# Mamba scan with a mixture-of-experts layer: z products in slot 9, the next x transposed in slot 58, the last state's quarters scaled by ScalarE and summed on TensorE

## The chip, the cores and the metric

The kernel runs on one core of one Trainium2 chip. The metric is the device time of one execution in microseconds. The core's engines are TensorE (PE; PEld is its weight load), VectorE (DVE), ScalarE (ACT), GpSimd (POOL) and SyncE (SP), which here issues all DMAs. Each engine runs its own list of instructions in order; semaphores tie the lists together.

## The reference

The input `x` is 2 sequences of 4096 tokens with 256 values. All is float32.

```python
x = x + layernorm(mamba(layernorm(x)))
x = x + layernorm(moe(layernorm(x)))

def mamba(x):                        # 512 inner channels, 16 states
    x_in, z = split(x @ W_in)
    u = silu(causal_conv(x_in, 4 taps) + conv_b)
    dt_lr, B, C = split(u @ W_xproj)            # 16, 16, 16
    delta = softplus(dt_lr @ W_dt + b_dt)
    A = -exp(A_log)
    h[n] = exp(delta * A[n]) * h[n] + delta * u * B[n]   # over time, for each of 16 states
    y = sum_n h[n] * C[n]
    return ((y + D_skip * u) * silu(z)) @ W_out

def moe(x):                          # 8 experts of width 128, top 2, and a shared one of 256
    coef = top-2 of softmax(x @ router)
    return shared(x) + sum_e coef[e] * (silu(x @ gate[e]) * (x @ up[e])) @ down[e]
```

## The kernel before, in words

The tokens are cut into 16 chunks of 512, 8 of each sequence, the two sequences taken in turn. Channels lie on the partitions: 512 channels are 4 blocks `j`, 512 tokens are 4 quarters `a` of 128. The kernel is a software pipeline. In body `s` the scan of chunk `s` runs; beside it run the output part and the experts of chunk `s-1` (`ffn_part`), the preparation of chunk `s+1` (`prep_part`: x and z products, convolution, delta, B, C), and the loading and normalising of `x` for chunk `s+2` (`XA`). Every body has 64 slots, and each engine's list is written out slot by slot: in slot `t` VectorE does scan `t` (state `t//4`, block `t%4`), and all other work is placed by slot numbers (`XIN_PE`, `YD_PE`, `Z_PE`, `SILU`, and so on). Nothing is planned at run time.

The scan itself: ScalarE computes `d_a = exp(delta * a)` into one of two PSUM banks (`decay`, L602, two slots ahead; it waits for the scan that last read the bank), POOL computes `d_bu` for two blocks at once (`inflow`, L987), VectorE runs the recurrence (`scan_step`, L753). When a state's 4 blocks are done, TensorE transposes each quarter into one of two `ht` banks (`transpose_state`, L445). The quarter is scaled by `C` and summed into `y_t`: the first state by ScalarE (`first_state`, L610), the other 15 by VectorE (`add_state`, L763), two in every second slot (`ADDS`), and the last state's four quarters in slots 0 and 1 of the next body (`ADDS_LATE`).

After that, in slots 2 to 9 of the next body, `y_t` is transposed back (`transpose_y`, L458, into two `RING` and two `DN` banks), VectorE adds `D_skip * u` (`skip_u`, L770, slot 3), POOL multiplies by silu(z) (`gate_y`, L1033, slot 4), TensorE projects (`project_out`, L469), VectorE takes moments (slot 8), POOL makes `rstd_o`, VectorE adds the stream and takes the next moments (slot 9, L786), ScalarE normalises (L619), TensorE transposes (L490), ScalarE copies to `x1_t` (L660). Each expert pair has a gate product, silu (L671, `silu_slot`: 14, 24, 34, 44, 52), up product, copy (L675), `hidden` on POOL (L1040, L1045) and a down product (L536) that accumulates in `DN`. In slot 60 VectorE takes the moments of y over `DN` (L774), before the adds of that slot; in slot 0 ScalarE normalises them (`normed_y`, L628), and POOL adds them to the stream (`add_stream_y`, L976, slot 7).

Preparation: `x_t` transposes the normalised `xa` (L423, slot 0), ScalarE copies it (L688, slot 1); x products (L433) go to the ring in slots 4, 7, 8; tap 0 on ScalarE (L698), the others on VectorE (L907); z products 0 and 1 in slot 9 into `DN`, 2 and 3 in slots 60 and 61 into the ring; silu of u and z (L704, L708) in slots 8, 11 and 62. ScalarE's `exp`, `silu` and `softplus` each need a table load where they follow one another; `Copy` and `Identity` don't.

Of the kernel before, what the change touches and what calls it, by code (L numbers as in the profile page):

```python
# [33 lines left out]
def mamba_moe_kernel(nc, x, w_in, conv_w, conv_b, w_xproj, w_dt, b_dt, a_log, d_skip, w_out,  # L34
# [3 lines left out]
    P = 128  # L38
# [20 lines left out]
    with ExitStack() as ctx:  # L59
# [51 lines left out]
        HF = sb("hidden", [P, 2, T])  # L111
        UP = sb("up", [P, 2, T])
# [41 lines left out]
        yd, y_first, xt = stage("yd", J), stage("y_first", NT), stage("xt", KM)  # L154
# [10 lines left out]
        scan, add_c, carry = stage("scan", NS * J), stage("add_c", (NS - 1) * NT), stage("carry_s", NS)  # L165
# [4 lines left out]
        conv, u_s, sz = stage("conv", J * TAPS), stage("u_s", J), stage("sz", J)  # L170
        RT_STEPS = 18
# [18 lines left out]
        YD_PE, YD_DVE, Y_GATE, OUT_PE = 2, 3, 4, (5, 5, 6, 6)  # L190
        Y_POOL = 7
# [12 lines left out]
        ADDS_LATE = {0: (SLOTS - NT, SLOTS - NT + 1), 1: (SLOTS - NT + 2, SLOTS - NT + 3)}  # L204
# [191 lines left out]
        def _(pe):  # L396
# [4 lines left out]
            def body(s, lo, r):  # L401
# [3 lines left out]
                for t in range(SLOTS):  # L405
# [3 lines left out]
                    for q in ADDS_LATE.get(t, ()):  # L409
                        if ffn:  # L410
                            transpose_state(s - 1, q)
                    if ffn:
                        ffn_part(s, lo, t)
                    if prep:
                        prep_part(s, lo, 1 - r, t)

            def x_t(s, lo):

                pe.wait_ge(norm["xa"].sem, norm["xa"].at(s + 1))
# [29 lines left out]
            def transpose_y(s, lo, j):  # L449

                pe.wait_ge(*added(s - 1, SLOTS - 1))
# [4 lines left out]
                bank = yd_bank(j)  # L456
                for a in range(NT):
                    last = nc.tensor.transpose(bank[:, a * P:(a + 1) * P],  # L458
                                               YT[:, a, j * P:(j + 1) * P], IDN[:, :])
# [82 lines left out]
            def prep_part(s, lo, o, t):  # L542
                c = s + 1
                if t == 0:
                    x_t(s, lo)
# [3 lines left out]
                for j in range(J):  # L549
                    if t == Z_PE[j]:  # L550
                        if j < 2:
                            pe.wait_ge(resid["o"].sem, resid["o"].at(s - 1, 2 * j + 2))
                        else:
                            pe.wait_ge(*ring_user_before(s, lo, "z", j))
                        for k in range(KM):
                            last = nc.tensor.matmul(z_bank(j)[:, :], WIN[:, k, DI + j * P:DI + (j + 1) * P],
# [31 lines left out]
        def _(act):  # L588
# [23 lines left out]

            def normed(w, c, dst, src):
# [18 lines left out]
            def body(s, lo, r):  # L632
                with_scan, ffn, prep = parts(lo)
                o = 1 - r
                for t in range(SLOTS):
# [47 lines left out]
            def prep_part(s, lo, o, t):  # L683
                c = s + 1
                if t == 1:
                    for k in range(KM):
                        act.wait_ge(full["xt"].sem, full["xt"].at(c, k + 1))
                        nc.scalar.activation(XT[:, k, :], ring_bank("xt", k)[:, :], ACT.Copy)\  # L688
# [398 lines left out]
```

## Time and profile before

| | |
|---|---|
| median of 3 runs | 2432.21 us (2432.09 to 2432.26) |
| profiled execution, its own time | 2430.07 us |
| span in the profile | 2428.1 us |
| VectorE busy | 2228.7 us, 92% |
| TensorE busy | 2073.8 us, 85% |
| GpSimd busy | 1906.6 us, 79% |
| ScalarE busy | 1601.1 us, 66% |

The span is cut into 40 slices on the page; VectorE stands at 9 tenths or more in all but the first and three of the last four. One chunk takes some 145.6 us (scan 0 of one at 1187.36 us, of the next at 1333.0 us). A line of the timeline view gives the start, the duration of a merged run of like instructions, and in brackets the idle time of that engine before it and what released it. A line without brackets followed the one before without a wait worth showing. In a merged run the instructions overlap a little: two adds of 0.73 us take 1.38.

### The profile page before, as it was taken

What the parts mean: (1) busy time and instruction counts of PE and PEld (TensorE: products, weight loads), DVE (VectorE), ACT (ScalarE), POOL (GpSimd) and SP (SyncE); (2) the same over time, 40 slices, a digit from 0 to 9 for tenths busy, and PEclk for the clock granted to TensorE, in tenths of its full rate; (3) what the DMA queues carried; (4) which work ended last, traced back from release to release, by engine and by line L of the source; (5) the groups of instructions that cost most, each with busy time, mean ns of one, the idle gap of its engine ahead of it and who ended that gap; (6) DMA issues with size and microseconds to landing.
All of it is one profiled execution on the core that took longest, in us unless ns stands there. A gap on an engine that the chain in (4) does not pass through costs nothing. (4 is left out here: it accounts for less than half of the span.)

```text
span 2428.1 us, 29696 instructions
## 1 busy us (share of the span) xinstructions
PE 2073.8 (85%) x8960; PEld 1322.8 (54%) x8960; DVE 2228.7 (92%) x3176; ACT 1601.1 (66%) x2358; POOL 1906.6 (79%) x1566
## 2 busy tenths in 40 slices
PE   5668989889898988989888898888989898896977
PEld 2445555656555555655655555555555555564544
DVE  3999999999999999999999999999999999998950
ACT  4556767676776767777677676667677676675632
POOL 3576887969789696978969788796978879698844
PEclk9659999999999999999999899999999999998989
DMA  4111211111121121111211121121112111111101
GB/s 135 34 34 42 70 53 57 58 49 57 53 62 57 49 57 58 57 53 58 65 46 47 58 65 55 55 57 50 56 53 62 61 49 53 49 57 48 65 23 44
DMA packets 92943, 134.23 MB, mean 55 GB/s; under 512 B 12000, under 2 KB 42976, under 8 KB 92784
## 3 DMA queue, kind: packets, MB, share of 16 engines
q1 hardware_dynamic: 92784, 132.34, 18.2%
q8 instruction: 72, 1.18, 0.2%
q14 instruction: 87, 0.71, 0.1%
HBM read 123.13 MB, written 9.18 MB: 54 GB/s over the span
## 5 line engine op out<-in xcount | busy, mean ns | idle before, releaser
L753 DVE TENSOR_TENSOR_SCAN h<-d_a,carry,d_bu 128x512 f32<-128x512 f32 x1024 | 1262.0, 1267 | 35.8 <-ACT d_a L602 35.4
L987 POOL TENSOR_TENSOR d_bu<-delta_u,b_rows 128x1024 f32<-128x1024 f32 x512 | 1202.3, 2357 | 5.1 <-DMA b_rows<-b_rows_hbm 0.9
L602 ACT ACTIVATE d_a<-delta,a_neg 128x512 f32<-128x512 f32 x1024 | 696.4, 689 | 622.2 <-DVE h L753 620.2
L445 PE MATMUL ht<-ident,h 128*128 128x128 f32 x4096 | 618.1, 295 | 116.8 <-DVE y_t L763 111.8
L445 PEld LDWEIGHTS ht<-ident,h 128*128 128x128 f32 x4096 | 503.7, 151 | 367.5 <-issue 132.0
L763 DVE SCALAR_TENSOR_TENSOR y_t<-ht,c_t,y_t 128x512 f32<-128x512 f32 x960 | 665.5, 734 | 2.8 <-PE ht L445 2.6
L509 PE MATMUL ring<-x_t,w_gate_sb 128*128 128x512 f32 x640 | 329.1, 641 | 20.6 <-ACT delta L718 19.1
L516 PE MATMUL ring<-x_t,w_up_sb 128*128 128x512 f32 x640 | 296.4, 606 | 23.0 <-ACT silu_gate L671 22.8
L536 PE MATMUL dn<-w_down_sb,hidden 128*128 128x256 f32 x1280 | 304.3, 381 | 13.2 <-POOL hidden L1045 13.2
L1040 POOL TENSOR_TENSOR hidden<-silu_gate,up 128x512 f32<-128x512 f32 x160 | 204.3, 1277 | 135.8 <-ACT up L675 77.9
L536 PEld LDWEIGHTS dn<-w_down_sb,hidden 128*128 128x128 f32 x1280 | 236.0, 190 | 74.8 <-issue 31.8
L1026 POOL TENSOR_TENSOR carry<-h,one 128x4 f32<-128x4 f32 x256 | 51.2, 200 | 238.7 <-DVE h L753 238.4
L516 PEld LDWEIGHTS ring<-x_t,w_up_sb 128*128 128x128 f32 x640 | 116.6, 191 | 151.7 <-issue 117.0
L602 ACT ACT_TABLE_LOAD x152 | 195.0, 1283 | 2.7
L509 PEld LDWEIGHTS ring<-x_t,w_gate_sb 128*128 128x128 f32 x640 | 121.3, 210 | 121.8 <-issue 90.7
L1045 POOL TENSOR_TENSOR hidden<-hidden,coef_rows 128x512 f32<-128x512 f32 x128 | 162.6, 1271 | 10.0
L907 DVE SCALAR_TENSOR_TENSOR u<-ring,conv_w_sb,u 128x511 f32<-128x511 f32 (+2 forms) x192 | 143.7, 748 | 6.8
L433 PE MATMUL ring<-x_t,w_in_sb 128*128 128x512 f32 x256 | 124.0, 629 | 17.7 <-DVE y_d L770 10.8
L469 PE MATMUL dn<-w_out_sb,y_d 128*128 128x256 f32 x512 | 114.5, 382 | 7.1 <-POOL y_d L1033 7.1
L774 DVE BATCH_NORM_STATS2 stats_o<-dn 128x6 f32<-128x256 f32 x128 | 45.4, 416 | 74.1 <-PE dn L536 65.4
L469 PEld LDWEIGHTS dn<-w_out_sb,y_d 128*128 128x128 f32 x512 | 96.0, 190 | 22.6 <-POOL y_d L1033 10.2
L675 ACT ACTIVATE up<-ring 128x512 f32<-128x512 f32 x160 | 92.8, 580 | 22.4 <-PE ring L516 22.4
(111 smaller groups left out, 1868.7 us busy)
## 6 DMA issues: line engine op xcount, KB each, us to landing
b_rows<-b_rows_hbm SPq DMA_DIRECT2D x256, 256.0 KB, 3.5
coef_rows<-coef_rows_hbm SPq DMA_DIRECT2D x128, 256.0 KB, 3.5
xa<-L_attn_x_in SPq DMA_DIRECT2D x16, 512.0 KB, 5.1
xr<-L_attn_x_in SPq DMA_DIRECT2D x16, 512.0 KB, 5.2
out<-xr SPq DMA_DIRECT2D x16, 512.0 KB, 2.9
w_in_sb<-L_attn_W_in_in SPq DMA_DIRECT2D x1, 1024.0 KB, 6.4
w_gate_sb<-L_ffn_experts_gate_in SPq DMA_DIRECT2D x2, 512.0 KB, 4.5
w_up_sb<-L_ffn_experts_up_in SPq DMA_DIRECT2D x2, 512.0 KB, 5.4
```

The costliest lines, as they stand in the source:

```text
L445: last = nc.tensor.transpose(HT[q % HTS][:, j * P:(j + 1) * P], H[:, (NS * c + n) % HS, j, a * P:(a + 1) * P], IDN[:, :])
L469: last = nc.tensor.matmul(DN[a // 2][:, (a % 2) * DM:(a % 2 + 1) * DM], YD[:, j, a * P:(a + 1) * P], WO[:, j, :], start=(j == 0 and a % 2 ...
L509: last = nc.tensor.matmul(bank[:, :], WG[:, k, f, :], X1T[:, k, :], start=(k == 0), stop=(k == KM - 1))
L516: last = nc.tensor.matmul(bank[:, :], WU[:, k, f, :], X1T[:, k, :], start=(k == 0), stop=(k == KM - 1))
L536: last = nc.tensor.matmul(DN[a // 2][:, (a % 2) * DM:(a % 2 + 1) * DM], HF[:, f % 2, a * P:(a + 1) * P], WD[:, f, :], start=(f == 0 and a ...
L602: nc.scalar.activation(DA[i % DAS][:, :], DL[:, r, j, :], ACT.Exp, scale=ANEG[:, j, n:n + 1]).then_inc(ex.sem, 1)
L753: nc.vector.tensor_tensor_scan(H[:, (NS * s + n) % HS, j, :], DA[(n * J + j) % DAS][:, :], BU[:, (2 * n + j // 2) % 4, j % 2, :], CARRY[:, ...
L763: nc.vector.scalar_tensor_tensor(YT[:, a, :], HT[q % HTS][:, :], CT[:, r, a, n:n + 1], YT[:, a, :], ALU.mult, ALU.add).then_inc(add_c.sem, 1)
L907: nc.vector.scalar_tensor_tensor(U[:, o, j, back:], bank[:, 0:T - back], CW[:, j, k:k + 1], U[:, o, j, back:], ALU.mult, ALU.add)\
L987: nc.gpsimd.tensor_tensor(BU[:, (2 * n + h) % 4, :, :], DU[:, 2 * h:2 * h + 2, :], BB[:, n % 2, :].unsqueeze(1).to_broadcast([P, 2, T]), A ...
L1040: nc.gpsimd.tensor_tensor(HF[:, f % 2, :], TG[:, f % 2, :], UP[:, f % 2, :], ALU.mult).then_inc(hf.sem, 1)
L1045: nc.gpsimd.tensor_tensor(HF[:, f % 2, :], HF[:, f % 2, :], CB[:, e % 2, :], ALU.mult)\
```

## The change

- `UP` and `HF` become halves of one tile `UP_HF` of `[P, 4, T]`, and the whole tile is also `YB`.
- The last state's four quarters are no longer added by VectorE. ScalarE scales them in slots 0 and 1 of the next body into `YB` (`last_state`), ahead of `normed_y` in slot 0. TensorE transposes `y_t` without closing the accumulation, then transposes `YB` onto it (`transpose_last`). `skip_u` moves from slot 3 to 4.
- All four z products stand in slot 9, in two `DN` banks in turn. ScalarE copies them as they are into `silu_z` (slots 8, 8, 9, 9 of its list) and applies silu in place, one in each of slots 24, 34, 44 and 52 (behind the gate silus there). For the first chunk all four silus stand in slot 11. The u silus of blocks 0 and 1 move from slot 8 to 7. The transposes of x1 wait for all four z copies.
- `x_t` moves from slot 0 to slot 58 of the body before, its copies to slot 59.
- On VectorE the moments of y stand behind the adds of slot 60; those of `xa` move from slots 32, 32, 42, 42 to 26, 32, 36, 42, with the aggregates in 46; POOL's `rstd_xa` moves to 47, ScalarE's normalisation to 50.
- On POOL the gates of slot 4 stand ahead of that slot's inflow, and `add_stream_y` moves from slot 7 to 8, behind `rstd_o`.

```diff
-        YD_PE, YD_DVE, Y_GATE, OUT_PE = 2, 3, 4, (5, 5, 6, 6)
-        Y_POOL = 7
+        YD_PE, YD_DVE, Y_GATE, OUT_PE = 2, 4, 4, (5, 5, 6, 6)
+        Y_POOL = 8
-        XA_STATS, XA_RSTD, XA_NORM = (32, 32, 42, 42), 44, 49
+        XA_STATS, XA_MEAN, XA_RSTD, XA_NORM, XT_PE, XT_ACT = (26, 32, 36, 42), 46, 47, 50, 58, 59
-        Z_PE, Y_STATS = (9, 9, 60, 61), 60
-        SILU = {8: [("u", 0), ("u", 1), ("z", 0), ("z", 1)], 11: [("u", 2), ("u", 3)], 62: [("z", 2), ("z", 3)]}
+        Z_PE, Z_ACT, Y_STATS = 9, (8, 8, 9, 9), 60
+        SILU = {7: [("u", 0), ("u", 1)], 11: [("u", 2), ("u", 3)], 24: [("z", 0)], 34: [("z", 1)],
+                44: [("z", 2)], 52: [("z", 3)]}
+        SILU_FIRST = {7: SILU[7], 11: SILU[11] + [("z", j) for j in range(J)]}
...
+            def transpose_last(s, j):
+                pe.wait_ge(*added(s - 1, SLOTS - 1))
+                for a in range(NT):
+                    last = nc.tensor.matmul(yd_bank(j)[:, a * P:(a + 1) * P], YB[:, a, j * P:(j + 1) * P], IDN[:, :],
+                                            start=False, stop=(a == NT - 1), is_transpose=True,
+                                            skip_group_check=True)
                 last.then_inc(full["yd"].sem, 1)
...
                 if t == X1T_PE:
                     if exists(lo + 1):
-                        pe.wait_ge(sz.sem, sz.at(s + 1, 2))
+                        pe.wait_ge(z_raw.sem, z_raw.at(s + 1))
...
+            def last_state(c, r, q):
+                a = q - SLOTS + NT
+                act.wait_ge(ht_full.sem, ht_full.at(c, q + 1))
+                act.wait_ge(down.sem, down.at(c - 1))
+                nc.scalar.activation(YB[:, a, :], HT[q % HTS][:, :], ACT.Copy, scale=CT[:, r, a, NS - 1:NS])\
+                  .then_inc(y_last.sem, 1)
...
+                for j in range(J):
+                    if t == Z_ACT[j]:
+                        act.wait_ge(full["z"].sem, full["z"].at(c, j + 1))
+                        act.wait_ge(y_gate.sem, y_gate.at(s - 1))
+                        nc.scalar.activation(SZ[:, o, j, :], DN[j % 2][:, :], ACT.Copy).then_inc(z_raw.sem, 1)
...
-                        nc.scalar.activation(SZ[:, o, k, :], z_bank(k)[:, :], ACT.Silu).then_inc(sz.sem, 1)
+                        act.wait_ge(z_raw.sem, z_raw.at(c, k + 1))
+                        nc.scalar.activation(SZ[:, o, k, :], SZ[:, o, k, :], ACT.Silu).then_inc(sz.sem, 1)
...
-                    for q in ADDS_LATE.get(t, ()):
-                        if ffn:
-                            add_state(s - 1, o, q)
```

## Rows read from the trace of the kernel before

**Rows 1.** The page's first part: busy us, share of the span, instructions.
```profile
PE 2073.8 (85%) x8960; PEld 1322.8 (54%) x8960; DVE 2228.7 (92%) x3176; ACT 1601.1 (66%) x2358; POOL 1906.6 (79%) x1566
```

**Rows 2.** Waits of VectorE, whole span: who for whom, us, times, longest.
```profile
DVE stats_o L774 <- PE dn L536: 65.4, 16, 47.4
DVE h L753 <- ACT d_a L602: 35.4, 78, 12.4
```

**Rows 3.** Timeline of VectorE inside a chunk: start, duration, instruction, [idle before <-releaser].
```profile
1113.26 2.46 DVE L753 TENSOR_TENSOR_SCAN h<-d_a,carry,d_bu 128x512 f32<-128x512 f32 x2 [0.20 <-ACT d_a L602]
...
1124.27 0.74 DVE L774 BATCH_NORM_STATS2 stats_xa<-xa 128x6 f32<-128x256 f32 x2
1124.93 2.44 DVE L753 TENSOR_TENSOR_SCAN h<-d_a,carry,d_bu 128x512 f32<-128x512 f32 x2
...
1144.32 0.38 DVE L780 BATCH_NORM_AGGREGATE mean_var_xa<-stats_xa 128x2 f32<-128x6 f32 x4
```

**Rows 4.** Timeline of VectorE at a chunk boundary.
```profile
1178.15 1.42 DVE L774 BATCH_NORM_STATS2 stats_o<-dn 128x6 f32<-128x256 f32 x4 [1.20 <-PE dn L536]
...
1184.87 1.27 DVE L753 TENSOR_TENSOR_SCAN h<-d_a,carry,d_bu 128x512 f32<-128x512 f32 x1
1186.06 1.38 DVE L763 SCALAR_TENSOR_TENSOR y_t<-ht,c_t,y_t 128x512 f32<-128x512 f32 x2
1187.36 1.27 DVE L753 TENSOR_TENSOR_SCAN h<-d_a,carry,d_bu 128x512 f32<-128x512 f32 x1
...
1194.71 1.38 DVE L770 SCALAR_TENSOR_TENSOR y_d<-u,d_skip_sb,ring 128x512 f32<-128x512 f32 x2
...
1212.45 1.66 DVE L786 SCALAR_TENSOR_TENSOR xr<-dn,rstd_o,xr 128x256 f32<-128x256 f32 x4 [1.30 <-POOL rstd_o L956]
...
1228.45 1.28 DVE L753 TENSOR_TENSOR_SCAN h<-d_a,carry,d_bu 128x512 f32<-128x512 f32 x1 [0.32 <-ACT d_a L602]
```

**Rows 5.** Timeline of ScalarE, inside a chunk and at the boundary.
```profile
1124.00 1.30 ACT L602 ACTIVATE d_a<-delta,a_neg 128x512 f32<-128x512 f32 x2
...
1189.32 1.91 ACT L628 ACTIVATE silu_gate<-dn,mean_rstd_y,rstd_y 128x256 f32<-128x256 f32 x4
...
1208.01 0.69 ACT L610 ACTIVATE y_t<-ht,c_t 128x512 f32<-128x512 f32 x1 [2.69 <-PE ht L445]
...
1214.04 1.15 ACT L704 ACTIVATE u<-u 128x512 f32<-128x512 f32 x2
...
1217.73 1.28 ACT L602 ACT_TABLE_LOAD   x1
...
1222.29 1.08 ACT L660 ACTIVATE x_t<-dn 128x512 f32<-128x512 f32 x2
...
1227.73 1.30 ACT L602 ACTIVATE d_a<-delta,a_neg 128x512 f32<-128x512 f32 x2
```

**Rows 6.** Timeline of TensorE at the boundary.
```profile
1176.12 1.99 PE L536 MATMUL dn<-w_down_sb,hidden 128*128 128x256 f32 x8 [0.82 <-POOL hidden L1045]
...
1195.57 3.67 PE L433 MATMUL ring<-x_t,w_in_sb 128*128 128x512 f32 x8 [1.08 <-DVE y_d L770]
...
1200.36 7.17 PE L469 MATMUL dn<-w_out_sb,y_d 128*128 128x256 f32 x32 [0.24 <-POOL y_d L1033]
1207.37 1.04 PE L445 MATMUL ht<-ident,h 128*128 128x128 f32 x8
```

**Rows 7.** Timeline of POOL at the boundary.
```profile
1188.11 2.36 POOL L987 TENSOR_TENSOR d_bu<-delta_u,b_rows 128x1024 f32<-128x1024 f32 x1
...
1199.03 4.98 POOL L1033 TENSOR_TENSOR y_d<-y_d,silu_z 128x512 f32<-128x512 f32 x4
...
1206.26 2.36 POOL L976 TENSOR_TENSOR xr<-xr,silu_gate 128x1024 f32<-128x1024 f32 x1
```

**Rows 8.** Timeline of VectorE in the first and the last scanned chunk.
```profile
54.91 7.26 DVE L753 TENSOR_TENSOR_SCAN h<-d_a,carry,d_bu 128x512 f32<-128x512 f32 x6 [3.12 <-ACT d_a L602]
...
2217.89 1.66 DVE L786 SCALAR_TENSOR_TENSOR xr<-dn,rstd_o,xr 128x256 f32<-128x256 f32 x4 [2.51 <-POOL rstd_o L956]
```

More of the change, by code:

```diff
@@ L110, in mamba_moe_kernel @@
         TG = sb("silu_gate", [P, 2, T])
-        HF = sb("hidden", [P, 2, T])
-        UP = sb("up", [P, 2, T])
+        UP_HF = sb("up_hidden", [P, 4, T])
+        UP, HF = UP_HF[:, 0:2, :], UP_HF[:, 2:4, :]
+        YB = UP_HF
         CB = sb("coef_rows", [P, 2, T])
@@ L408, in body @@
                             transpose_state(s, q)
-                    for q in ADDS_LATE.get(t, ()):
+                    for q in LAST_Q.get(t, ()):
                         if ffn:
@@ L549, in prep_part @@
                 for j in range(J):
-                    if t == Z_PE[j]:
+                    if t == Z_PE:
                         if j < 2:
@@ L642, in body @@
                         first_state(s, r, t - NT - 1)
+                    for q in LAST_Q.get(t, ()):
+                        if ffn:
+                            last_state(s - 1, o, q)
                     if exists(lo - 2) and t == 0:
@@ L650, in body @@
                         normed("xa", s + 2, XA, XA)
+                    if exists(lo + 2) and t == XT_ACT:
+                        for k in range(KM):
+                            act.wait_ge(full["xt"].sem, full["xt"].at(s + 2, k + 1))
+                            act.wait_ge(full["z"].sem, full["z"].at(s + 1))
+                            nc.scalar.activation(XT[:, k, :], ring_bank("xt", k)[:, :], ACT.Copy)\
+                              .then_inc(xt.sem, 1)
             def ffn_part(s, lo, o, t):
@@ L684, in prep_part @@
                 c = s + 1
[L685 to L688, printed above, removed]
-                          .then_inc(xt.sem, 1)
                 for j in range(J):
@@ L700, in prep_part @@
                           .then_inc(tap0.sem, 1)
-                for what, k in SILU.get(t, ()):
+                for j in range(J):
+                    if t == Z_ACT[j]:
+                        act.wait_ge(full["z"].sem, full["z"].at(c, j + 1))
+                        act.wait_ge(y_gate.sem, y_gate.at(s - 1))
+                        nc.scalar.activation(SZ[:, o, j, :], DN[j % 2][:, :], ACT.Copy).then_inc(z_raw.sem, 1)
+                for what, k in (SILU if exists(lo) else SILU_FIRST).get(t, ()):
                     if what == "u":
@@ L814, in body @@
                             moments("xa", s + 2, a, XA[:, a, :])
-                            if a == NT - 1:
-                                moments_end("xa", s + 2)
+                    if exists(lo + 2) and t == XA_MEAN:
+                        moments_end("xa", s + 2)
+                    if ffn and t == Y_STATS:
+                        dve.wait_ge(down.sem, down.at(s - 1))
+                        for a in range(NT):
+                            moments("y", s - 1, a, dn(a))
+                        moments_end("y", s - 1)
             def over(t):
@@ L885, in ffn_part @@
                             route(c, 8 * half + 2 + i)
-                if t == Y_STATS:
-                    dve.wait_ge(down.sem, down.at(c))
-                    for a in range(NT):
-                        moments("y", c, a, dn(a))
-                    moments_end("y", c)
             def conv_part(c, o, t):
@@ L999, in body @@
                         keep_state(s, r, n - 1)
-                    if with_scan and n + 1 < NS and t % 2 == 0:
-                        inflow(s, n + 1, t % NT // 2)
-                    if ffn and t == 60:
-                        rstd_of("y", s - 1)
                     if ffn and t == Y_GATE:
@@ L1006, in body @@
                             gate_y(s - 1, o, j)
+                    if with_scan and n + 1 < NS and t % 2 == 0:
+                        inflow(s, n + 1, t % NT // 2)
+                    if ffn and t == Y_STATS:
+                        rstd_of("y", s - 1)
                     if ffn and t == O_STATS:
```

39 lines of the change are left out of this document (18 added, 21 removed).

## The prediction

> **What bounds the kernel now.** I read the page's busy line first: VectorE is busy 92% of the span, the others 85% and less [rows 1]. Then who waits for whom: of VectorE's idle time 65.4 us stand before the moments over `dn` (47.4 of them once, in the tail) and 35.4 before scans that wait for ScalarE's decay exponentials [rows 2]. Then the engines' timelines around one chunk boundary, since only there can a wait be priced. I call decay(i) the exponential that scan i needs. ScalarE has two banks for it, so decay(i) can't start before scan i-2 has ended, and ScalarE runs its list in order: whatever stands between two decays on it must fit in the time that VectorE spends between two scans.
>
> Inside a chunk VectorE goes through two scans (2.46) and two adds (1.38) per two slots and hardly waits [rows 3, 4]. Where ScalarE has two silus between table loads (load 1.28, two silus 1.1, load 1.28, decay 0.7 [rows 5]), it comes 0.19 to 0.20 late [rows 3]. This is in slots 27, 37, 47 and 55 of every chunk. So ScalarE at 66% busy is, in these windows, already the one that ends last. At the boundary VectorE waits 1.20 for the last down product, 1.30 for `rstd_o` and 0.32 for decay(14) [rows 4]. I count time there from scan 63's start, 1184.87.
>
> **The change part by part.**
>
> 1. *Four adds a chunk leave VectorE.* Two take 1.30 between starts (1186.06, the first pair in slot 63, to scan 0 at 1187.36 [rows 4]), so 2.6 us a chunk, 42 in all. They turn into four ScalarE copies of about 0.6 a piece (0.69 long, 0.6 from start to start, like the decays [rows 5]) and 16 more TensorE transposes, 1.04 per 8 [rows 6]. The new accumulating transpose isn't in the trace; the nearest row is the plain one, the bound is 0 (hidden) to 2.1 us a chunk, and I take it as 2.1 that lie beside scan 4.
>
> 2. *Moments of y after the adds in slot 60.* The adds of slot 60 fill the 1.20 wait for the down product, so scan 63 starts at -1.25. Bounds: 0 to 1.25; I take 1.25, since nothing else holds those adds (their transposes, the work of slot 59, are done before TensorE gets to its 0.82 wait for POOL's last `hidden` [rows 6]).
>
> 3. *Slots 0 to 4.* Scan 0 then starts at 1.24. Scan 2 needs POOL's second inflow for the new chunk, which ends at 5.60 (1188.11 + 2.36 [rows 7]). POOL shows no wait ahead of it nor ahead of the gates, so it comes no earlier: scan 2 runs 5.65 to 6.9. ScalarE, from scan 0's end at 2.5: decay(2), two last-state copies, four normalisations (1.91 long, 1.83 to the next start [rows 5]), decay(3), two copies, decay(4): 0.6 + 1.2 + 1.8 + 0.65 + 1.2 + 0.7, so decay(4) ends near 8.6. Scan 4 runs 8.65 to 9.9 and the skips begin at 9.85. In before they began at 9.84 with one scan fewer done. Of the 3.9 us saved (parts 1 and 2) 1.2 are left on VectorE at this point; 2.7 have become waits for POOL and ScalarE.
>
> 4. *Slots 4 to 9.* TensorE's x products start when the first skip is done, 10.65 against 10.70 before [rows 6]. After them come two transposed states and the out-projection (7.17), which waited 0.24 for POOL's gates and won't now, since the gates are ahead of an inflow (11.9 instead of 14.16 [rows 7]). So the transposes at 22.50 come at 22.25, and ScalarE's third first-state copy at 22.9 instead of 23.14 [rows 5]. VectorE is at the x1 work about 2 us earlier than in before, its wait for `rstd_o` down from 1.30 to 0.2, as `add_stream_y` (2.36) now stands behind it on POOL. None of this matters if ScalarE is later than that.
>
> 5. *Slots 7 to 14 on ScalarE, the piece that decides.* Before, from 23.14: copy, decay(10), copy, two tap-0s, load, two silus, two z silus, load, decay(11), four normalisations, decay(12), two X1T copies, decay(13), load, two silus, load, decay(14) at 42.86 [rows 5]. It had some 2.5 us idle between these, waiting for x and z products. After, from 22.9: copy, load 1.28, silus 1.15, load 1.28, decay(10) at 27.3, copy to 28.6, tap-0s to 30.0. TensorE's fifth and sixth states wait for that copy, so z products run 29.1 to 36.5 (1.85 each; the x products, of the same shape, take 3.67 for two [rows 6]). z copies 0 and 1 end at 31.6 and 33.4, decay(11) at 34.1, normalisations at 36.0, z copies 2 and 3 at 37.1, decay(12) 37.8. TensorE's transposes of x1 wait for the fourth z copy: 37.1 to 38.2 instead of overlapping the normalisations; X1T copies to 39.3, decay(13) 39.9, load, silus, load, decay(14) starts at 43.7. Against 42.86 that is 0.85 later. VectorE, with less to do, waits about 2.6 us for it. So a boundary costs +0.85 net, though VectorE has 2.6 us less work in it. Bounds: all of the 3.9 us gained, -3.9, if VectorE stays last; +2.1 if the 1.25 of part 2 isn't had. Nearest to the rows: +0.85. Boundaries with all three parts are 14 (chunks 1 to 14 scanning): +12.
>
> 6. *One more silu in slots 24, 34, 44, 52.* Each adds 0.57 (two from SBUF to SBUF take 1.15 [rows 5]) in the window that is already 0.19 late. Moved VectorE work fills a part: one of the xa moments (0.74 for two) now stands in slots 26 and 36, the aggregates (0.38) in 46 [rows 3]. So waits of 0.39, 0.39, 0.38, 0.76 for four of 0.19: +1.16. The moments leave slots 32 and 42, where softplus stands between two loads: decay(33) ended at 1124.69, its scan started at 1124.93 [rows 3, 5], and without 0.37 of cover it waits about 0.17; the same is taken for slot 43: +0.34. Sum +1.5 for each of 13 chunks, +2.3 in chunk 14's, where no xa is left to move, nothing in chunk 0's, which has no gate silus: +22. Bounds 0 and +2.8 a chunk.
>
> 7. *The silus of slot 62 go*, and with them two table loads a chunk (2.56 us of ScalarE). No scan waited there (scan 1 started 1.1 us after its decay), so 0, except once: chunk 0's scan 1 waited 3.12 for just these [rows 8].
>
> 8. *x transposed in slots 58 and 59* instead of 0 and 1: 1.04 on TensorE ahead of its 0.82 wait, 1.08 on ScalarE, where two decays of 0.7 are all that it has in 3.7 us: 0. It frees 1.1 us of ScalarE in slot 1, already counted. The load of the next `xa` still goes out in slot 2: 0.
>
> 9. *Ends.* Ahead of chunk 0 everything is serial. The u silus of slot 7 now hold back the third tap 0 (+1.4), four z copies and silus stand ahead of the copy of `x_dbl` (+2.6), the x transposes ahead of decay(0) (+1.7), and the 3.12 of part 7 go: about +2.8 by scan 14. Bounds -1 and +6. The last scanned chunk has no z work: gates and `rstd_o` are about 2 us earlier and the wait of 2.51 [rows 8] mostly goes: -2.5. Tail: normalisations between the last-state copies cost about what part 2 gives: 0.
>
> **Sum.** 12 + 22 + 2.8 - 2.5 = +34. The profiled span of 2428.1 becomes 2462; the profiled execution's own 2430.07, 2464. The median of the runs shown, 2432.21, is 2.1 above it; scaled with it: **2466 us**, 1.4% slower. Its own range, with a boundary off by 1.4 us either way: 2445 to 2486.
>
> **Rivals.**
>
> *A, VectorE stays the bound (faster).* For it: 92% busy, and 2.6 + 1.25 us a boundary taken off it. Against it: the walk of part 5, in which ScalarE has 1.1 us more copies and waits for four z products in a row. It wins if decay(14) can start 2.3 us or more before the old 42.86, say because the third first-state copy comes that much earlier. With the full 3.9 kept at 14 boundaries and part 6 paid: -54 + 22 = -32, and with the ends at 0, 2400. The Trainium skill (Perfetto Trace Analysis, "Optimizing Scalar/DVE Operations") says that moving work to the Scalar engine may make sense when DVE is saturated, and ScalarE: Activation LUTs, "Rules for kernel authors", says to group functions by table set. By these two the copies and the shared loads of parts 6 and 7 are gains. The trace agrees that two loads of 1.28 go, but shows that no scan waited for them. Chance 0.20.
>
> *B, it evens out.* Part 6 as computed, the boundary at -1.5: within 5 us of 2432. Chance 0.08.
>
> *C, the slot-60 swap gives nothing,* because POOL or TensorE holds the adds: parts 3 to 5 all 1.25 later, +17: 2484. For it: TensorE's transposes of slot 61 follow the down product. Chance 0.14.
>
> *D, the change as forecast,* 0.58.
>
> **How the numbers follow.** No change and a change can be told apart here at about 0.2%, 5 us. Faster 0.20 (A), same 0.08 (B), slower 0.72 (C and D). The range reaches from the middle of A to C: 2412 to 2486; outside are half of A and the worst of C.
>
> **What would show it.** VectorE busy down by 42 to 47 us with the span up. Waits of scans for decays up from 35 to over 100 us: of 0.4 to 0.8 in slots 27, 37, 47, 55, of 1 to 2 in slots 2 to 4, and one over 2 us at scan 14. The wait for the down product in slot 60 and that for `rstd_o` nearly gone. If the wait at scan 14 is under 0.5 us, part 5 is wrong and A is right; if slots 27 to 55 still show 0.2, part 6 is.

## The result, and the profile after

| | before | after |
|---|---|---|
| median | 2432.15 us (2431.85 to 2432.26, 4 runs) | 2454.41 us (2453.86 to 2455.24, 4 runs) |
| span in the profile | 2428.1 us | 2452.1 us |
| scan 14's wait for decay(14), per chunk | 0.32 us | 2.73 us |
| one chunk, from one x1 moments to the next | 143.95 us mean, 143.75 where nothing disturbs it | 145.44 us mean |

The ratio of after to before is 1.0092, 95% interval [1.0075, 1.0109]: slower by 0.9%. The forecast was 2466 with a range of 2412 to 2486, and slower was its likeliest case. The 145.6 us given for one chunk ahead of the prediction is wrong: scan 0 of the next chunk starts at 1331.10 us, 143.74 behind 1187.36. No term of the prediction uses it.

The page's first part of the changed kernel, to be held against [rows 1]:

```profile
PE 2106.0 (86%) x9216; PEld 1376.5 (56%) x9216; DVE 2190.8 (89%) x3112; ACT 1638.5 (67%) x2462; POOL 1909.1 (78%) x1566
```

VectorE has 37.9 us less work, and the span is 24 us longer: 62 us more of VectorE's time are waits. The waits of VectorE over the whole span (who for whom, us, times, longest) name them; the first two rows answer to [rows 2]:

```profile
DVE h L780 <- ACT d_a L613: 95.8, 101, 17.7
...
DVE stats_o L801 <- PE dn L549: 47.4, 1, 47.4
DVE h L780 <- POOL d_bu L1011: 29.5, 14, 2.1
```

Waits for decays went from 35.4 to 95.8 us. The down product is waited for only in the tail (65.4 to 47.4). A wait that before did not have, for POOL's second inflow, appears 14 times. In the timeline of VectorE inside a chunk, each of the four windows that showed 0.19 to 0.20 in [rows 3] now shows its one silu more:

```profile
1127.76 2.46 DVE L780 TENSOR_TENSOR_SCAN h<-d_a,carry,d_bu 128x512 f32<-128x512 f32 x2 [0.38 <-ACT d_a L613]
...
1138.76 0.42 DVE L801 BATCH_NORM_STATS2 stats_xa<-xa 128x6 f32<-128x256 f32 x1
1139.22 2.46 DVE L780 TENSOR_TENSOR_SCAN h<-d_a,carry,d_bu 128x512 f32<-128x512 f32 x2
...
1147.36 2.46 DVE L780 TENSOR_TENSOR_SCAN h<-d_a,carry,d_bu 128x512 f32<-128x512 f32 x2 [0.38 <-ACT d_a L613]
...
1166.96 2.46 DVE L780 TENSOR_TENSOR_SCAN h<-d_a,carry,d_bu 128x512 f32<-128x512 f32 x2 [0.42 <-ACT d_a L613]
...
1182.43 2.46 DVE L780 TENSOR_TENSOR_SCAN h<-d_a,carry,d_bu 128x512 f32<-128x512 f32 x2 [0.71 <-ACT d_a L613]
```

The timeline of VectorE at the boundary, against [rows 4]; the prediction's clock zero, old scan 63's start, is 1200.08 here, as scan 63 starts at 1198.83, 1.25 before it:

```profile
1192.14 1.38 DVE L790 SCALAR_TENSOR_TENSOR y_t<-ht,c_t,y_t 128x512 f32<-128x512 f32 x2
1193.44 1.42 DVE L801 BATCH_NORM_STATS2 stats_o<-dn 128x6 f32<-128x256 f32 x4
...
1198.83 1.28 DVE L780 TENSOR_TENSOR_SCAN h<-d_a,carry,d_bu 128x512 f32<-128x512 f32 x1
...
1205.87 2.46 DVE L780 TENSOR_TENSOR_SCAN h<-d_a,carry,d_bu 128x512 f32<-128x512 f32 x2 [2.10 <-POOL d_bu L1011]
1208.71 1.28 DVE L780 TENSOR_TENSOR_SCAN h<-d_a,carry,d_bu 128x512 f32<-128x512 f32 x1 [0.39 <-ACT d_a L613]
1209.91 1.38 DVE L797 SCALAR_TENSOR_TENSOR y_d<-u,d_skip_sb,ring 128x512 f32<-128x512 f32 x2
...
1225.50 1.66 DVE L813 SCALAR_TENSOR_TENSOR xr<-dn,rstd_o,xr 128x256 f32<-128x256 f32 x4 [0.30 <-POOL rstd_o L980]
...
1244.02 1.28 DVE L780 TENSOR_TENSOR_SCAN h<-d_a,carry,d_bu 128x512 f32<-128x512 f32 x1 [2.73 <-ACT d_a L613]
```

The boundary's gain is given back at three places: 2.10 for POOL and 0.39 for ScalarE ahead of the skips, 2.73 at scan 14. ScalarE's timeline in the same stretch (against [rows 5]) shows what stands ahead of decay(14), the two table loads around the silus of u last:

```profile
1222.71 0.69 ACT L621 ACTIVATE y_t<-ht,c_t 128x512 f32<-128x512 f32 x1 [3.35 <-PE ht L449]
...
1230.93 0.60 ACT L728 ACTIVATE silu_z<-dn 128x512 f32<-128x512 f32 x1 [1.00 <-PE dn L567]
1232.65 0.60 ACT L728 ACTIVATE silu_z<-dn 128x512 f32<-128x512 f32 x1 [1.12 <-PE dn L567]
...
1237.85 1.09 ACT L688 ACTIVATE x_t<-dn 128x512 f32<-128x512 f32 x2 [0.49 <-PE dn L503]
...
1239.54 1.28 ACT L732 ACT_TABLE_LOAD   x1
1240.83 1.15 ACT L732 ACTIVATE u<-u 128x512 f32<-128x512 f32 x2
1242.00 1.28 ACT L613 ACT_TABLE_LOAD   x1
1243.30 1.30 ACT L613 ACTIVATE d_a<-delta,a_neg 128x512 f32<-128x512 f32 x2
```

And TensorE and POOL there, against [rows 6, 7]: 16 z matmuls in one piece, the x1 transposes behind the fourth z copy, and POOL's inflow of 2.36 that ends at 5.7 on the clock:

```profile
1229.02 7.03 PE L567 MATMUL dn<-x_t,w_in_sb 128*128 128x512 f32 x16
1236.84 1.09 PE L503 MATMUL dn<-ident,up_hidden 128*128 128x128 f32 x8 [0.79 <-ACT silu_z L728]
```

```profile
1203.41 2.36 POOL L1011 TENSOR_TENSOR d_bu<-delta_u,b_rows 128x1024 f32<-128x1024 f32 x1
```

### The profile page after: what moved, and what is told of

The parts are those of the page before. It is cut to its first block and busy times, and to the rows that moved or that the text cites. A ratio compares the mean times of both kernels' runs of the same rounds, so it can differ in the third digit from the quotient of the medians.

```text
span 2452.1 us, 30280 instructions
## 1 busy us (share of the span) xinstructions
PE 2106.0 (86%) x9216; PEld 1376.5 (56%) x9216; DVE 2190.8 (89%) x3112; ACT 1638.5 (67%) x2462; POOL 1909.1 (78%) x1566
## 5 line engine op out<-in xcount | busy, mean ns | idle before, releaser
L780 DVE TENSOR_TENSOR_SCAN h<-d_a,carry,d_bu 128x512 f32<-128x512 f32 x1024 | 1263.3, 1268 | 129.0 <-ACT d_a L613 95.8
L449 PE MATMUL ht<-ident,h 128*128 128x128 f32 x4096 | 630.5, 299 | 205.0 <-DVE y_t L790 159.1
L449 PEld LDWEIGHTS ht<-ident,h 128*128 128x128 f32 x4096 | 516.6, 153 | 433.1 <-DVE y_t L790 179.5
L790 DVE SCALAR_TENSOR_TENSOR y_t<-ht,c_t,y_t 128x512 f32<-128x512 f32 x896 | 621.3, 735 | 0.1
L529 PE MATMUL ring<-x_t,w_up_sb 128*128 128x512 f32 x640 | 308.4, 626 | 14.7 <-ACT silu_gate L699 14.2
L1064 POOL TENSOR_TENSOR up_hidden<-silu_gate,up_hidden 128x512 f32<-128x512 f32 x160 | 204.5, 1278 | 145.4 <-ACT up_hidden L703 91.9
L549 PE MATMUL dn<-w_down_sb,up_hidden 128*128 128x256 f32 x1280 | 304.3, 381 | 13.2 <-POOL up_hidden L1069 13.2
L549 PEld LDWEIGHTS dn<-w_down_sb,up_hidden 128*128 128x128 f32 x1280 | 235.9, 190 | 74.9 <-issue 31.8
L1069 POOL TENSOR_TENSOR up_hidden<-up_hidden,coef_rows 128x512 f32<-128x512 f32 x128 | 162.7, 1271 | 10.0
L567 PE MATMUL dn<-x_t,w_in_sb 128*128 128x512 f32 x256 | 112.5, 592 | 0.0
L703 ACT ACTIVATE up_hidden<-ring 128x512 f32<-128x512 f32 x160 | 93.1, 582 | 24.8 <-PE ring L529 24.5
```

The costliest lines, as they stand in the source:

```text
L449: last = nc.tensor.transpose(HT[q % HTS][:, j * P:(j + 1) * P], H[:, (NS * c + n) % HS, j, a * P:(a + 1) * P], IDN[:, :])
L529: last = nc.tensor.matmul(bank[:, :], WU[:, k, f, :], X1T[:, k, :], start=(k == 0), stop=(k == KM - 1))
L549: last = nc.tensor.matmul(DN[a // 2][:, (a % 2) * DM:(a % 2 + 1) * DM], HF[:, f % 2, a * P:(a + 1) * P], WD[:, f, :], start=(f == 0 and a ...
L780: nc.vector.tensor_tensor_scan(H[:, (NS * s + n) % HS, j, :], DA[(n * J + j) % DAS][:, :], BU[:, (2 * n + j // 2) % 4, j % 2, :], CARRY[:, ...
L790: nc.vector.scalar_tensor_tensor(YT[:, a, :], HT[q % HTS][:, :], CT[:, r, a, n:n + 1], YT[:, a, :], ALU.mult, ALU.add).then_inc(add_c.sem, 1)
L1064: nc.gpsimd.tensor_tensor(HF[:, f % 2, :], TG[:, f % 2, :], UP[:, f % 2, :], ALU.mult).then_inc(hf.sem, 1)
```

## The experiments

Each starts from the kernel before or the changed one ("after") and is given with its ratio to runs of before taken beside it. In the diffs three dots stand for lines that aren't shown; edits that only rename semaphores aren't shown either, nor always the old place of lines that move. The labels e1, e2 and so on are those that the expectations use.

### The two orders alone, together (e1) and one by one (e12, e13)

```diff
-        Y_POOL = 7
+        Y_POOL = 8
...
                     for q in ADDS_LATE.get(t, ()):
                         if ffn:
                             add_state(s - 1, o, q)
+                    if ffn and t == Y_STATS:
+                        dve.wait_ge(down.sem, down.at(s - 1))
+                        for a in range(NT):
+                            moments("y", s - 1, a, dn(a))
+                        moments_end("y", s - 1)
...
+                    if ffn and t == Y_GATE:
+                        for j in range(J):
+                            gate_y(s - 1, o, j)
                     if with_scan and n + 1 < NS and t % 2 == 0:
                         inflow(s, n + 1, t % NT // 2)
```

> The kernel before, with only the order changed: moments of y behind the adds of slot 60, POOL's gates ahead of the inflow of slot 4, add_stream_y in slot 8 behind rstd_o. Theory 1 (the order of the lists at the boundary decides): the waits of 1.20 and 1.30 us a chunk go, 2.5 us in each of 14 to 15 chunks, 35 us: 2395 to 2400. Theory 2 (VectorE's busy time decides, waits are made up elsewhere): no work is taken away, so 2432.

2398.2 us (2397.02 to 2399.45), ratio 0.9863 [0.9849, 0.9878]. As expected, and faster than both kernels. A chunk where nothing disturbs it takes 141.45 us, 2.3 less than before's 143.75 and 3.9 less than the changed kernel's 145.37. The changed kernel contains both orders, so the rest of it cost 56 us, not 22. Of the 3.9, 2.4 are the longer wait at scan 14 (0.33 here) and 1.3 the stretch from scan 14 to slot 60. The two halves of the edit were then run apart.

> The kernel before with one edit: the moments of y behind the adds of slot 60. It splits the 33 us that the orders alone gave. Theory 1: the two orders are independent, the wait of 1.20 for the down product goes and nothing downstream takes it back: 1.2 us x 14 = -17, 2415 us (2410 to 2420), wait for rstd_o still 1.3. Theory 2: VectorE only arrives earlier at the wait for rstd_o, which grows to 2.5: no change, 2428 to 2435.

2431.49 us, ratio 0.9998 [0.9989, 1.0007]: theory 2, with the wait that it named. The wait of 1.20 for the down product was gone and turned into 1.2 more at the wait for `rstd_o`. VectorE of this kernel:

```profile
1211.95 1.66 DVE L786 SCALAR_TENSOR_TENSOR xr<-dn,rstd_o,xr 128x256 f32<-128x256 f32 x4 [2.53 <-POOL rstd_o L956]
```

> The kernel before with POOL's order alone: gates of slot 4 ahead of that slot's inflow, add_stream_y in slot 8 behind rstd_o. Theory 1: the wait for rstd_o falls from 1.3 to 0.3 and that for decay(14), 0.32, goes too or stays: -1.0 to -1.3 us x 14 = -14 to -18, 2414 to 2418 us. Theory 2 (the orders work only together): 2428 or more.

2420.04 us, ratio 0.9951 [0.9934, 0.9967]. The wait for `rstd_o` fell from 1.30 to 0.30 as theory 1 has it, and the chunk where nothing disturbs it is 142.76 long, 1.0 less. Others took 143.4 to 143.7, with more waits of adds for a transposed state (6.3 us in 15 times over the span, against 2.6 in 6 before), so the total is 2 us above the 2414 to 2418 expected. VectorE:

```profile
1209.12 1.66 DVE L786 SCALAR_TENSOR_TENSOR xr<-dn,rstd_o,xr 128x256 f32<-128x256 f32 x4 [0.30 <-POOL rstd_o L956]
...
1256.62 1.41 DVE L763 SCALAR_TENSOR_TENSOR y_t<-ht,c_t,y_t 128x512 f32<-128x512 f32 x2 [0.48 <-PE ht L445]
```

Alone the edits gave 0 and 12 us, together 34. In before, the wait for `rstd_o` is set by POOL's list from the boundary on, not by when VectorE comes: VectorE 1.2 earlier only waits 1.2 longer there, until POOL's list is reordered too.

### The swap of slot 60 undone in the changed kernel (e10)

```diff
+                    if ffn and t == Y_STATS:
+                        dve.wait_ge(down.sem, down.at(s - 1))
+                        for a in range(NT):
+                            moments("y", s - 1, a, dn(a))
+                        moments_end("y", s - 1)
                     if prep:
                         conv_part(s + 1, o, t)
...
-                    if ffn and t == Y_STATS:
...
-                        moments_end("y", s - 1)
```

> The changed kernel, with the moments of y ahead of the adds of slot 60, as before. Theory 1: VectorE waits 1.2 us for the down product again, everything up to decay(14) starts 1.25 later, the waits after it are the same except that for POOL in slot 2 (2.1 to 0.9): +1.2 us in 14 chunks, 2471 (2465 to 2476). Theory 2 (POOL's inflow of slot 62 sets the time of all that follows, so the wait only moves): 2454.

2475.01 us (2473.95 to 2476.12), ratio 1.0177 [1.0162, 1.0192]. The chunk is 146.68 long, 1.24 more than after's 145.44: the swap is worth its whole 1.25 there, and rival C, which had it give nothing, is refuted. Over the whole kernel it is worth 20.6 us, 3 more than 14 times 1.25; most of these 3 stand in the last scanned chunk and behind it.

### The last state's adds on VectorE again (e2)

```diff
                     for q in LAST_Q.get(t, ()):
                         if ffn:
-                            last_state(s - 1, o, q)
...
+                    for q in LAST_Q.get(t, ()):
+                        if ffn:
+                            add_state(s - 1, o, q)
...
-                    for j in range(J):
-                        transpose_last(s, j)
```

> The changed kernel, with the last state's four quarters added by VectorE again in slots 0 and 1 (no second tile, no 16 extra transposes, no last-state copies on ScalarE); z products, slots and orders as changed. Theory 1: in the changed kernel VectorE waits 2.1 us for POOL and 0.4 for ScalarE in slots 2 to 4; the four adds (2.6 us) fill just these waits, so the time stays within 5 us of 2454. Theory 2 (VectorE's busy time decides): +2.6 us in 15 chunks, 2493. Theory 3 (the extra ScalarE copies and transposes are what made the change slower): back by 10 us or more, under 2445.

2475.56 us (2473.54 to 2476.38), ratio 1.0181 [1.0164, 1.0198]. It lies between the theories. The skips start 8.52 us after scan 0, in after 8.59: the four adds fill exactly the waits of 2.10 and 0.39, so on VectorE alone parts 1 and 3 cancel. What differs is on TensorE, where no theory had looked. This is its timeline at two boundaries of this kernel:

```profile
1217.81 1.97 PE L461 MATMUL ring<-ident,y_t 128*128 128x128 f32 x8 [1.18 <-DVE y_t L786]
...
1222.08 3.67 PE L437 MATMUL ring<-x_t,w_in_sb 128*128 128x512 f32 x8 [0.59 <-DVE y_d L794]
...
1363.09 1.09 PE L461 MATMUL ring<-ident,y_t 128*128 128x128 f32 x8 [1.19 <-DVE y_t L786]
...
1367.36 5.37 PE L437 MATMUL ring<-x_t,w_in_sb 128*128 128x512 f32 x8 [2.30 <-DVE y_d L794]
```

The windows view has the clock of both. The third figure from the end is the granted clock of the stretch, behind the five engines' busy times; 1.00 is the level of 2.4 GHz, 0.50 that of 1.2 GHz, and what lies between is a mixture:

```profile
1210.00:1222.00 12.00, 9.23 (x40) 7.66 (x38) 12.00 (x15) 5.93 (x10) 11.32 (x18) 0.51 0.20 65
1222.00:1226.00 4.00, 3.92 (x12) 1.99 (x13) 4.00 (x5) 1.56 (x4) 4.00 (x5) 1.00 0.20 59
1355.00:1363.00 8.00, 5.83 (x24) 4.67 (x24) 8.00 (x11) 3.88 (x7) 7.55 (x12) 0.58 0.00 1
1363.00:1367.00 4.00, 1.97 (x16) 1.73 (x16) 4.00 (x5) 1.77 (x3) 3.77 (x8) 1.00 0.74 177
1367.00:1373.00 6.00, 5.64 (x12) 2.60 (x13) 5.93 (x9) 1.73 (x4) 6.00 (x6) 0.72 0.39 126
```

The low level stands at both boundaries; what differs is what falls into it. At the first it lasts through the transposes of `y_t` (1.97 per 8), and the x products have the full clock. At the second it ends before these transposes (1.09), which leaves an idle stretch of 2.30, and the x products behind that run at 0.72. The idle time right ahead does not decide it: at two other boundaries the same products took 5.55 and 6.10 us behind only 0.59 and 0.60, with the clock still at 0.50 when they began (starts 194.02 and 486.47). They took over 5 us at 10 of the 14 boundaries and 3.67 at 4. In after they took 3.60 or 3.67 at all 14.

Inside this one kernel the two kinds can be compared. From the first skip to scan 14 it takes 34.11 us where the x products are fast, just as in after (1209.91 to 1244.02), and 35.80 at most of the slow ones, 35.99 and 36.54 at the two named. Over the ten that makes 18 of the 21 us between this kernel and after. VectorE sees a part of it as new waits for the out-projection, 0.43 to 0.97 at each slow boundary. So theory 1 was right wherever the x products had the full clock, and most of what the last state's move gains over this kernel lies at the boundaries where they hadn't.

Then, in that kernel, each transpose of `y_t` was made twice (`transpose_y`, e7):

```diff
-                for a in range(NT):
+                for a in range(2 * NT):
+                    a %= NT
```

> The kernel of e2 (adds back on VectorE), with each of the 16 transposes of y_t done twice into the same place, so TensorE is as busy ahead of the x products as in the changed kernel, with no other difference. In e2 the two x products of slot 4 took 5.37 us after 2.30 us of idle TensorE at some boundaries, 3.67 in the changed kernel, and the moments over the out-projection waited 0.8 us for it. Theory 1 (TensorE's clock falls in that idle time, and this is most of e2's distance from the changed kernel): x products 3.67 again, the wait of 0.8 gone, 2463 (2458 to 2468), faster with more work. Theory 2 (e2 is slower for its VectorE work alone): 2475 or more.

2475.54 us (2474.13 to 2477.09), ratio 1.0180 [1.0163, 1.0197]: a miss of theory 1 in time, nothing gained over the kernel above, though its first half came true. Theory 2 has the number, but not its reason, as the fast boundaries above show. The x products took 3.60 or 3.67 at all 14 boundaries, so with work in the gap the clock stayed up for them; but the doubled transposes stand at the low clock themselves, at most boundaries they end 1.2 to 1.4 us later than the x products could otherwise have started, and at five boundaries a skip waited 0.19 to 0.24 for them:

```profile
1215.51 3.68 PE L462 MATMUL ring<-ident,y_t 128*128 128x128 f32 x16 [1.18 <-DVE y_t L787]
1218.98 2.39 PE L462 MATMUL dn<-ident,y_t 128*128 128x128 f32 x16
1221.20 3.60 PE L437 MATMUL ring<-x_t,w_in_sb 128*128 128x512 f32 x8
```

From the first skip to scan 14 it now takes 35.1 to 35.5 us at 13 of the 14 boundaries, more than the fast kind above and less than the slow one: the filling costs about what the clock gives back.

### The orders and the last state, without the rest (e8)

```diff
                 if t == YD_PE:
                     for j in range(J):
                         transpose_y(s, lo, j)
+                    for j in range(J):
+                        transpose_last(s, j)
...
+                    for q in ADDS_LATE.get(t, ()):
+                        if ffn:
+                            last_state(s - 1, o, q)
...
-                    for q in ADDS_LATE.get(t, ()):
-                        if ffn:
-                            add_state(s - 1, o, q)
```

The kernel with the two orders, and in it the last state on ScalarE and TensorE as in the change (`last_state` stands in ScalarE's list); x_t stays in slot 0, its copies in slot 1, the skips in slot 3, z products and silus where before has them.

> The kernel of e1 (before, with only the order changed), and the last state's quarters scaled by ScalarE and summed on TensorE as in the change; z products, silus and x transposes stay where they were before. Theory 1 (ScalarE's chain orders the boundary): VectorE's 2.6 us of adds become waits, 2400 (2393 to 2412). Theory 2 (VectorE at 92% busy is the bound): 2398 - 42 = 2356, at least under 2380.

2466.68 us (2465.54 to 2467.35), ratio 1.0143 [1.0128, 1.0159]: 68 us slower than the two orders alone, where the expectation had it level. VectorE waits 4.96 at the skips (74.7 us over the span). First TensorE of this kernel, then ScalarE:

```profile
1211.40 1.94 PE L460 MATMUL ring<-ident,y_t 128*128 128x128 f32 x8 [3.51 <-ACT x_t L711]
1213.13 1.92 PE L460 MATMUL dn<-ident,y_t 128*128 128x128 f32 x8
1214.84 1.91 PE L467 MATMUL ring<-ident,up_hidden 128*128 128x128 f32 x8
```

```profile
1205.95 1.24 ACT L630 ACTIVATE up_hidden<-ht,c_t 128x512 f32<-128x512 f32 x2
1207.09 1.92 ACT L648 ACTIVATE silu_gate<-dn,mean_rstd_y,rstd_y 128x256 f32<-128x256 f32 x4
...
1209.49 1.28 ACT L630 ACTIVATE up_hidden<-ht,c_t 128x512 f32<-128x512 f32 x2
1210.63 1.11 ACT L711 ACTIVATE x_t<-ring 128x512 f32<-128x512 f32 x2
```

The x_t copies stand behind the last state's copies and the normalisations. The transposes of `y_t` need the ring banks that these copies free, and wait 3.51; then 24 of the 32 transposes run at about 1.92 per 8 instead of 1.04. The granted clock of that stretch was 0.57, after 3.5 us without a matmul. So in this arrangement the last state's move costs 4.9 us a boundary (68 over 14), and the trace lays the wait on the x_t copies; x_t in slot 58 (part 8) is no free passenger. A kernel that differs from this one in the place of x_t alone was not run, so how much of the 68 us that slot gives back is not shown.

### Where the z silus stand

```diff
-                for what, k in (SILU if exists(lo) else SILU_FIRST).get(t, ()):
+                for what, k in SILU_FIRST.get(t, ()):
```

All four behind the u silus of slot 11, in every chunk (e3).

> The changed kernel, with all four z silus in slot 11 behind the u silus, in the load that stands there, in place of slots 24, 34, 44, 52. Theory 1: 2.17 us more in ScalarE's chain to decay(14), so the wait at scan 14 grows from 2.73 to 4.9; the waits in slots 27, 37, 47 (0.38, 0.38, 0.42) go and the one in 55 is 0.2 instead of 0.71: +2.2 - 1.7 = +0.5 us a chunk, 2461 (2455 to 2467). Theory 2: ScalarE does the same work in both, 2454, and no wait at scan 14 near 5 us.

2466.56 us (2465.04 to 2467.26), ratio 1.0144 [1.0128, 1.0159], within theory 1's range. The windows' waits in slots 27, 37 and 47 are gone, that at 55 is 0.20, and what they held, four silus of 0.57, comes back at scan 14: 4.81 instead of 2.73.

```profile
1253.06 1.28 DVE L780 TENSOR_TENSOR_SCAN h<-d_a,carry,d_bu 128x512 f32<-128x512 f32 x1 [4.81 <-ACT d_a L613]
```

```diff
-        SILU = {7: [("u", 0), ("u", 1)], 11: [("u", 2), ("u", 3)], 24: [("z", 0)], 34: [("z", 1)],
-                44: [("z", 2)], 52: [("z", 3)]}
+        SILU = {7: [("u", 0), ("u", 1)], 11: [("u", 2), ("u", 3)], 60: [("z", j) for j in range(J)]}
```

All four in slot 60, in every chunk but the first (e4).

> The changed kernel, with all four z silus in slot 60 between two table loads of their own (2.56 us more of ScalarE a chunk). Theory 1: slot 60 has the moments of y on VectorE as cover (load 1.3, four silus 2.2, load 1.3, decay 0.7 and the decay before it 0.65 are 6.1 us against 6.8 of VectorE's work), so no new wait there, and the waits of slots 27 to 55 fall from 1.9 to 0.2 a chunk: -1.7 us in 14 chunks, 2430. The rule that functions are to be grouped by table set, taken by itself: two more loads a chunk, so slower, 2454 + 36 if they were on the path.

2437.41 us (2435.93 to 2439.0), ratio 1.0023 [1.0014, 1.0033]. Two loads more in every chunk, and 17 us faster than after: there ScalarE has room. It is 7 us above the 2430 expected: the chunk is 1.5 shorter (1.7 expected), a wait for the down product came back in 12 chunks (0.17 to 0.45, 4.8 us in all), and in chunk 0, which has no moments of y as cover in slot 60, a scan waits 1.71 for its decay. Part 6 of the prediction, priced at 1.5 a chunk, is confirmed in size from the other side.

### Two z products out of slot 9 (e5 and e9)

```diff
-        Z_PE, Z_ACT, Y_STATS = 9, (8, 8, 9, 9), 60
+        Z_PE, Z_ACT, Y_STATS = (9, 9, 56, 56), (8, 8, 57, 57), 60
...
-                        pe.wait_ge(z_raw.sem, z_raw.at(s + 1))
+                        pe.wait_ge(z_raw.sem, z_raw.at(s + 1, 2))
```

Both are built on the kernel above, with the z silus in slot 60. Products 2 and 3 go to the ring; the diff is that of the first kernel (e5), in the second (e9) they stand in slots 20 and 21, their copies in 21 and 22.

> The kernel of e4, with z products 2 and 3 in slot 56 into the ring (copied by ScalarE in slot 57) instead of in slot 9, so that the x1 transposes wait for two z copies, not four. Theory 1 (ScalarE's chain from the third first-state copy to decay(14) ends last): it loses 1.1 us of copies and the transposes of x1 overlap the normalisations again, so decay(14) is 1.8 us earlier, the wait at scan 14 falls from 2.73 to about 0.9: -1.8 us in 14 chunks, 2411 (2404 to 2418). Theory 2 (the wait at scan 14 is made up by another, from POOL or the down product): 2430 or more.

2449.88 us (2448.27 to 2450.89), ratio 1.0074 [1.0059, 1.0089]: theory 1 missed by 39 us.

> The kernel of e5, with z products 2 and 3 in slots 20 and 21 (copied in 21 and 22) instead of 56. In e5 the wait at scan 14 fell from 2.73 to 1.18, but the products stood ahead of the transposes of slot 57, and two adds waited 1.91 us for these. Theory 1 (the chain to decay(14) is shorter by what e5 showed, and only the new place was bad): the 1.91 goes, the wait at scan 14 stays at 1.2 or under, 145.4 - 1.5 (e4) - 1.5 = 142.4 us a chunk, 2415 (2408 to 2425). Theory 2 (the two z products cost TensorE as much wherever they stand): 2440 to 2450.

2445.92 us (2444.72 to 2446.56), ratio 1.0058 [1.0041, 1.0075]: its theory 2, and 31 us above its theory 1. The wait at scan 14 fell from 2.73 to 1.18 to 1.27 in both, where 0.9 and at most 1.2 were reckoned. But the z matmuls in a row (eight of 0.45 us in slot 56, four of 0.46 in each of slots 20 and 21) hold up TensorE's transposes of states, and VectorE's adds wait for those. In slot 56 the wait is long (1.9); with slots 20 and 21 it comes three or four times a chunk (0.72, 0.54 and 0.21 in the chunk shown). VectorE of the first kernel, then of the second:

```profile
1187.79 1.41 DVE L793 SCALAR_TENSOR_TENSOR y_t<-ht,c_t,y_t 128x512 f32<-128x512 f32 x2 [1.92 <-PE ht L452]
...
1242.88 1.28 DVE L783 TENSOR_TENSOR_SCAN h<-d_a,carry,d_bu 128x512 f32<-128x512 f32 x1 [1.18 <-ACT d_a L616]
```

```profile
1119.89 1.41 DVE L792 SCALAR_TENSOR_TENSOR y_t<-ht,c_t,y_t 128x512 f32<-128x512 f32 x2 [0.72 <-PE ht L451]
...
1240.02 1.28 DVE L782 TENSOR_TENSOR_SCAN h<-d_a,carry,d_bu 128x512 f32<-128x512 f32 x1 [1.26 <-ACT d_a L615]
```

A version with z products and silus as before, x_t in slot 58 and the last state moved wasn't tried: there z products 2 and 3 of slots 60 and 61 would read the x_t that slot 59 overwrites.

## Why the prediction was right

The sign and the mechanism were right: VectorE gave up 3.85 us of work and waiting at a boundary, and ScalarE's list up to decay(14) took them. The size was too high: the profiled span grew by 24 us, not 34, and the median lies 12 us under the forecast. Measured in four intervals: the head +2.2 us, 13 chunks of +1.49, the last scanned one +2.4, the tail +0.1, together 24.1.

1. *Part 1.* VectorE busy fell by 37.9 us, not 42 to 47. The 64 adds are 41.6 of it (0.65 each); four lone moments a chunk at 0.42 in place of two pairs at 0.74 [rows 3] give back 0.2 in each of 14 chunks, 2.8.
2. *Part 2* was right only together with the POOL order: 1.24 a chunk in the changed kernel, nothing in before with VectorE's order alone. The prediction named POOL's gates in part 4, but gave them no share of the gain.
3. *Part 3* was right nearly to the row: skips at 9.83 on the clock (forecast 9.85), 2.10 and 0.39 of waiting, which the forecast had as "2.7 have become waits". Its last paragraph, though, looked for waits of 1 to 2 us for decays in slots 2 to 4; only 0.39 is for a decay, the 2.10 is for POOL, so all waits for decays came to 95.8 us and not to over 100. And one thing went well by luck: the forecast priced all transposes at 1.04 per 8, but of those of `y_t` ahead of the skips the first eight took 1.5 to 1.9 at the low clock here too (granted 0.75 from 1204.0 to 1210.7). They ended in time, the skips came late for it by 0.48 at the first boundary and by at most 0.16 at the others, and the x products behind had the full clock. The kernel with the adds back shows what that is worth.
4. *Part 4.* `rstd_o` is waited for 0.30 (forecast 0.2), and the skips' successors come some 2.1 earlier.
5. *Part 5* is the term that was mis-sized. decay(14) starts at 43.22 on the clock against 43.7: from the scans of slot 59 to scan 14 it is 53.95 before (1174.50 to 1228.45) and 54.24 after (1189.78 to 1244.02), +0.29 instead of +0.85. Over 14 boundaries 4 us instead of 12. ScalarE's list ran in the order forecast. TensorE's z products took 7.03 in a row against 7.4 reckoned (1.85 each, from a row of two) and ended at 35.97 on the clock (1229.02 and 7.03) against 36.5; the second z copy, which waits for its product, ended at 33.2 against 33.4. The rest of the 0.5 is spread over the rows behind.
6. *Part 6.* The four waits are 0.38, 0.38, 0.42 and 0.71 (forecast 0.39, 0.39, 0.38, 0.76). The 0.34 for softplus didn't come: a lone moment holds VectorE 0.46 (1138.76 to 1139.22), where the pair held it 0.66 [rows 3], so 0.20 of cover went and not 0.37, and the margin there was 0.24 (1124.69 to 1124.93). The chunk apart from the boundary is 1.33 longer instead of 1.5, and the last one's middle 2.07 instead of 2.3: 19 us instead of 22.
7. *Part 7* was right: no scan before waited there, and the 3.12 of chunk 0 [rows 8] is gone.
8. *Part 8* was priced at 0, and no wait in its slots speaks against that. What it is worth was never asked: in the one kernel that moves the last state without it, that move makes the orders alone 68 us slower.
9. *Part 9.* Scan 14 of chunk 0 stands 2.6 later (88.75 against 86.2); the forecast's own terms add up to 2.6 too (1.4 + 2.6 + 1.7 - 3.12), though it wrote 2.8. In the last scanned chunk the boundary is 2.2 shorter (forecast 2.5), though by another wait than thought: that for `rstd_o` only went from 2.51 to 1.86, that of the moments for the out-projection, 2.05, is gone, and scan 8 waits 1.91.

By the prediction's own terms this is 4 + 19.4 + 2.6 - 2.2 = 24, to the nearest us.

Rival A needed a wait under 0.5 at scan 14; it was 2.73. What part of A was right shows in the orders alone: the 34 us were there for the taking, and 2398 us is what A had reckoned (2400) for the whole change. The Trainium skill (Perfetto Trace Analysis, "Optimizing Scalar/DVE Operations") says that moving work to the Scalar engine may make sense when DVE is saturated, and here DVE was at 92%. The runs agree only as far as ScalarE has room in the same stretch. At the boundary it had none: the span grew though VectorE's busy time fell by 37.9 us. The Trainium skill (ScalarE: Activation LUTs, "Rules for kernel authors") also says to group functions by table set. The change did that and spared 2 loads a chunk; putting two loads back beside slot 60 made the kernel 17 us faster, so here the place of a silu outweighed its load.

In six experiments theory 1 missed by more than 10 us: the adds put back, the transposes doubled, the last state alone, the z products in slot 56, those in slots 20 and 21, and the moments' order alone. For the last two kernels theory 2, named beforehand, came true. Each time one engine's list had been reckoned through and the miss stood on another: on POOL's for the moments, on TensorE in the other five, as its clock, as transposes behind longer work, or as a wait for banks.

## What to carry to other kernels

Work that leaves the busiest engine is worth what the next wait on it allows: walk every other engine's list to the next point where they meet, and look there first for a mere reordering, which here gave 34 us, while the moved work on top of it cost 56. Two reorderings on two engines may only pay as a pair: alone they gave 0 and 12 us. An operation that shares banks with a moved one belongs to the move.

## What the hardware showed that was not expected

- TensorE's clock fell within a boundary, in a kernel where TensorE is busy for 85% of the span and more. Eight x products took 3.67 us at a granted clock of 1.00 and 5.37 at 0.72, the latter after an idle of 2.30; but also 5.55 and 6.10 after idles of 0.59 and 0.60, where the stretch ahead was already at 0.50. Eight transposes took 1.04 at full clock and 1.92 in a stretch of 0.57, after an idle of 3.51.
- Filling an idle stretch with repeated transposes left the products behind at full speed (3.60), but the filling itself ran 3.68 us for its first 16 transposes.
- A moment that stands alone on VectorE takes 0.46 us from start to the next start, one of a pair 0.33.
